# Adding a fixed 256x256 position matrix to an attention product: on VectorE, or on TensorE through the identity

## What is computed

```python
prod2 = jnp.einsum('bnt,btm->bnm', lhs2, rhs2)             # 256x16 times 16x256, per sample
S = jnp.einsum('kj,bij->bik', V_s, jax.nn.sigmoid(prod2 + b_s))   # b_s: 256x256, one for all samples
S = jax.nn.softmax(S, axis=1)
for k in range(3):
    r = jnp.einsum('mn,bmn,bmft->bnft', cheb[k], S, x)
    out = out + jnp.einsum('bnft,fo->bnot', r, Theta[k])
```

## Time and profile before

| what | value |
| --- | --- |
| runs | 702.01, 700.87, 695.55 us; median 700.87 us |
| profiled execution | 696.03 us, span 694.0 us, 12572 instructions |
| mean granted TensorE clock | 0.911 of full |
| busy share of the span | TensorE 80%, weight loads 52%, VectorE 59%, ScalarE 36%, GpSimd 31% |
| L1149, the add of `bs` | 16 times, 678 ns each, 83.2 to 339.7 us |
| L741, the tanh | 16 times, 616 ns each, 83.9 to 342.6 us |
| L459, the product | 64 records, 374 ns each |

### The profile page before, as it was taken

One profiled execution on the slowest core, in us unless ns is written; L12 is line 12 of the kernel. 1 busy time (PEld: TensorE's weight loads), 2 busy tenths in 40 slices (PEclk: granted clock), 3 DMA queues, 4 the chain that ended last, 5 costly groups with the idle time before them and its releaser, 6 DMA issues. The chain is left out here.

```text
span 694.0 us, 12572 instructions
## 1 busy us (share of the span) xinstructions
PE 555.2 (80%) x2488; PEld 362.5 (52%) x2489; DVE 409.3 (59%) x1809; ACT 251.8 (36%) x619; POOL 213.7 (31%) x283
## 2 busy tenths in 40 slices
PE   0567599999999999999985225999999999999243
PEld 0233357766666666666663102666666666665122
DVE  4645236888888888988889771333333333332255
ACT  0343144345544444445442110333333333333232
POOL 5000001224333444443345440334334433443100
PEclk9989599999999999999999556999999999999655
DMA  9900000000000000000001032222222222221597
GB/s 299 421 4 1 0 1 1 0 1 32 31 30 30 31 30 30 30 23 23 27 27 55 31 106 70 77 85 83 84 85 91 78 85 87 91 83 42 164 321 240
DMA packets 36247, 52.69 MB, mean 76 GB/s; under 512 B 4606, under 2 KB 31361, under 8 KB 35969
## 3 DMA queue, kind: packets, MB, share of 16 engines
q1 hardware_dynamic: 24816, 30.86, 14.3%
q0 software_dynamic: 6480, 16.85, 6.5%
q10 hardware_dynamic: 4928, 4.72, 2.1%
HBM read 30.19 MB, written 23.14 MB: 77 GB/s over the span
## 5 line engine op out<-in xcount | busy, mean ns | idle before, releaser
L619 PE MATMUL bank<-w,xT 128*128 x284 | 135.9, 601 | 2.1 <-DVE xT L1420 2.1
L1420 DVE COPY xT<-bank 128x256 f32<-128x256 f32 x71 | 30.2, 425 | 143.8 <-PE bank L606 143.8
L975 POOL DMA_INDIRECT yrows<-xT,dest x71 | 69.4, 978 | 139.4 <-ACT xT L831 135.3
L496 PE MATMUL bank<-work 128*128 128x256 f32 x384 | 93.3, 386 | 0.0
L944 POOL DMA_INDIRECT xrows<-xtok,slot x64 | 64.3, 1005 | 81.4 <-DVEq L1315 66.7
L932 POOL TENSOR_TENSOR yg<-work,sml 128x512 f32<-128x512 f32 x16 | 18.0, 1122 | 196.3 <-DVE work L1225 193.0
L496 PEld LDWEIGHTS bank<-work 128*128 128x128 f32 x384 | 70.4, 190 | 9.0 <-issue 0.8
L634 PE MATMUL bank<-w,xT 128*128 x284 | 73.3, 380 | 1.6 <-ACT xT L836 1.6
L619 PEld LDWEIGHTS bank<-w,xT 128*128 128x128 f32 x284 | 48.8, 192 | 37.6 <-issue 37.6
L825 ACT ACTIVATE xT<-bank 128x256 f32<-128x256 f32 x71 | 27.4, 386 | 94.9 <-PE bank L619 94.9
L634 PEld LDWEIGHTS bank<-w,xT 128*128 128x128 f32 x284 | 48.5, 190 | 6.2 <-issue 2.6
(11 more groups left out here) (203 smaller groups left out, 1017.9 us busy)
## 6 DMA issues: line engine op xcount, KB each, us to landing
xT<-xrows SPq DMA_DIRECT2D x71, 129.0 KB
xT<-yrows SPq DMA_DIRECT2D x32, 256.0 KB, 3.9
xs<-x_in SPq DMA_DIRECT2D x4, 1024.0 KB, 10.8
w<-w13t_in SPq DMA_DIRECT2D x1, 4096.0 KB, 18.3
out<-xT ACTq DMA_DIRECT2D x16, 256.0 KB, 3.7
w<-w2t_in SPq DMA_DIRECT2D x1, 2048.0 KB, 22.7
yrows<-xT,dest POOLq DMA_INDIRECT x71, 2.4
xrows<-xtok,slot POOLq DMA_INDIRECT x64
```

Source lines behind the costliest of these rows:

```text
L496: last = mm(bank[6][:, h * N:(h + 1) * N], z[:, p, c, k, h], A[:, p, c, k], start=(c == 0 and k == 0), stop=(c == C - 1 and k == K - 1))
L619: last = mm(bank[2 + q][:, :], xc[:, q, c], w13[:, e, c].rearrange("p w n -> p (w n)"), start=(c == 0), stop=(c == C - 1))
L975: pool.indirect_dma_start(yrows, bass.IndirectOffsetOnAxis(ap=dest[:, q], axis=0), yo[:, q], None, bounds_check=2 * TOKENS - 1, oob_is_err ...
L1420: V.tensor_copy(xc[:, q].rearrange("p c k -> p (c k)"), bank[q][:, 0:C * P]).then_inc(c_xc, 1)
```

## The change

In `product` each of the two halves of `bank[1]` gets a second matmul: the 128x128 identity times the 128x256 chunk of `bs` opens the accumulation group and the product of `lr` closes it. `add_bs` and its semaphore `b_bs` are gone from VectorE. ScalarE's tanh waits for the product, reads `bank[1]` in PSUM and writes `sg`; it stands ahead of `normalise` in ScalarE's list. The wait on the logits of sample `b-2`, which protects the buffer `sg`, moves from VectorE to ScalarE.

```diff
@@ product, TensorE
                 for c in range(C):
+                    mm(bank[1][:, c * N:(c + 1) * N], ident, bs[:, c], start=True, stop=False)
                     last = mm(bank[1][:, c * N:(c + 1) * N], lr[0:T, p, N + c * P:N + (c + 1) * P],
-                              lr[0:T, p, 0:N], start=True, stop=True)
+                              lr[0:T, p, 0:N], start=False, stop=True)
@@ tanh, ScalarE
             def tanh(b, p):
-                act.wait_ge(s["b_bs"], done(b))
-                nc.scalar.activation(sg[:, p], sg[:, p], ACT.Tanh, scale=0.5).then_inc(s["b_th"], 1)
+                act.wait_ge(s["b_pr"], done(b))
+                act.wait_ge(s["b_L"], done(b - 2))
+                nc.scalar.activation(sg[:, p].rearrange("p c n -> p (c n)"), bank[1][:, :], ACT.Tanh, scale=0.5).then_inc(s["b_th"], 1)
@@ turn, ScalarE
+                if ahead2:
+                    tanh(i + 2, q)
                 if back2:
                     normalise(i - 2, q)
-                if ahead2:
-                    tanh(i + 2, q)
@@ VectorE
-            def add_bs(b, p):
-                dve.wait_ge(s["b_pr"], done(b))
-                dve.wait_ge(s["b_L"], done(b - 2))
-                V.tensor_tensor(sg[:, p].rearrange("p c n -> p (c n)"), bank[1][:, :],
-                                bs[:].rearrange("p c n -> p (c n)"), ALU.add).then_inc(s["b_bs"], 1)
-                yield
@@ matrices in turn, VectorE
                         yield from weigh(i + 1, 1 - q)
-                    if ahead2:
-                        yield from add_bs(i + 2, q)
```

More of the change, by code:

```diff
@@ L246, in build @@
         a_ec = sem("a_ec"); a_rep = sem("a_rep"); a_gh = sem("a_gh")
-        names = ("b_gh b_lr b_pr b_bs b_th b_L b_max b_exp b_rec b_pn b_tr b_A b_z b_zc b_main b_relu b_conv "
+        names = ("b_gh b_lr b_pr b_th b_L b_max b_exp b_rec b_pn b_tr b_A b_z b_zc b_main b_relu b_conv "
                  "b_y b_cen b_sq b_var b_dn b_x1 b_st b_g1 b_q b_g2 b_nb b_xn b_tk b_tkc b_gt b_gtc b_lg "
@@ L992, in _ @@
             V = nc.vector
-            for n in "b_gb b_bs b_max b_rec b_A b_y b_cen b_var b_dn b_st b_q b_nb b_sh b_M b_slot".split():
+            for n in "b_gb b_max b_rec b_A b_y b_cen b_var b_dn b_st b_q b_nb b_sh b_M b_slot".split():
                 dve.sem_inc(s[n], START)
```

## The result

The kernel after takes 710.73 us in the median of four runs (709.12 to 713.29), against 700.66 us for the kernel before in the same comparison: ratio 1.0186, interval 1.0151 to 1.0222. It is slower by 1.9%, about 13 us; the interval holds 2%, so on which side of 2% it lies stays open. The profiled execution took 709.12 us, 13.09 us over the one of before.

A forecast was written before the change was run, and what follows sets the result against it. VectorE's loop was taken to bound steady turns by 0.17 and 0.38 us over TensorE; 1.1 + 2.7 + 0.1 + 0.9 + 3.8 = +8.6 us, added to 698.6, gave 707.2 us, range 700 to 712.

The forecast's parts named there:

- the price of the identity calls: TensorE, each turn's product group: four more matmul records cost 0.90 us, with 0.88 and 1.06 as bounds.
- The third rival: Product group: calls alternating two heights of weights cost the product's 1.06 us; +11.3 us, 709.9 us; chance 0.13.
- Turns -1 to 1: First turns of part B, with no gap on TensorE: 0.9 us more each, +2.7 us.
- turn -2: Start of part B at half clock: 1.8 us for four more records, less 0.7 for the earlier tanh, +1.1 us.
- The steady turn: Turns 4 to 13: +0.26 us in odd turns (18.41) and +0.5 in even (19.23), 3.8 us in all.
- the forecast's loop: Steady turns: route_c through row_max, ScalarE's exps and scale, turn_softmax, features and prefix back to route_c; 18.41 and 19.23 us.
- Turn 2: Part B: TensorE's 0.81 us wait before tokens takes all but 0.1 of the 0.9 us; +0.1 us.
- turn 3: Part B: prefix starts with no wait at all, so the new calls cost their full price, +0.9 us.
- The first rival: Steady turns: VectorE sets the turn and TensorE's gaps take the new calls; -1.8 us, 696.8 us; chance 0.13.
- The second rival: Steady turns: TensorE's own loop alone sets the turn, as scale comes in time; +1.8 us, 700.4 us; chance 0.12.
- The turn is VectorE's loop: Kernel before, steady turns: one route_c to the next sets the turn, by 0.17 us in odd and 0.38 in even turns.
- The tanh: ScalarE: starting off PSUM instead of SBUF, ahead of normalise, costs nothing and is worth nothing in steady turns.

The follow-up runs named there:

- `one_call`: The kernel after with both halves of bs in one identity call of 512 columns ahead of the product calls; ratio to the kernel before 1.0116, about +8 us.
- `both_adds`: The kernel before with the two identity calls added and VectorE's add kept, so bs is added twice; ratio to the kernel before 1.0173.
- `no_add`: The kernel after without the two identity calls, so the position matrix is left out; ratio to the kernel before 0.9904, -6.7 us.
- `after_early`: The kernel after with prefix moved up in TensorE's list to just behind the product; ratio to the kernel before 1.0007.
- `before_early`: The kernel before with prefix moved up in TensorE's list to just behind the product; ratio to the kernel before 0.9978.
- `tanh_late`: The kernel after with the tanh put back behind normalise in ScalarE's list; ratio to the kernel before 1.0151.
- `before_full`: The kernel before with the product over all 128 rows, the added rows being zero; ratio to the kernel before 1.0015.

## Why the prediction was wrong

The direction and the chain of causes came out; the size of the change didn't: 13 us against a sum of 8.6, and against the 6.3 us between the forecast time, 707.2, and the median shown, 700.87. That the measured 710.73 lies in 700 to 712 is luck in part: the ratio of 1.0186 on the comparison's own 700.66 would be 713.7.

- **The step that failed is the price of the identity calls**: "I take 0.90 us a turn, with 0.88 and 1.06 as bounds". Its columns cost the 0.87 of the rows; two more changes of height brought the whole to 3.70 - 2.44 = 1.26 us, outside both bounds. `one_call`, where the same columns come without the two changes (0.86 us), lost 8.1 us, close to the forecast's 8.6. The upper bound was the product's own 1.06, which was read as the price of low calls. It is the price of a group with a change on either side: 0.86 without. The third rival named the alternation but gave it that price too; its sign, a group of 2.1 us and more, was met with 2.41. Turns -1 to 1 show the term bare, 1.12 to 1.25 us each for 0.9. In turn -2, at half clock, the group grew by 2.6 us (4.67 for 2.07) and not by 1.8, which made 1.84 of the expected 1.1.
- **The steady turn was right in kind.** The longer wait of `route_c` (1.6 us for 1.1 to 1.4), `prefix` with no wait ahead of it, L479 waiting for L757 in both kinds of turn and `both_adds` all show the forecast's loop. With 1.26 for 0.90 its sums are 18.77 and 19.59 us for a measured 18.72 and 19.42. The ten turns lost 6.3 us, not 3.8. Turn 2 lost 0.37 for 0.1 and turn 3 1.07 for 0.9; with 1.26 they would be 0.46 and 1.26. The whole sum with 1.26 in it is 14.8 us for a measured 13.1, so what else stands in it is a little too high, by 1.7 us over 16 turns.
- **The first rival** (TensorE's gaps take the calls) fell: `both_adds` equals the kernel after. The Trainium skill's "Perfetto Trace Analysis", section "Identifying the Most-Contended Engine", led to it by reading TensorE at its weight-load share, 67% against VectorE's 89%. VectorE does matter, and its instruction is worth 6.7 us by itself (`no_add`); what decided was TensorE's gap at the place that counts, 0.17 us ahead of `prefix`.
- **The second rival** (TensorE's own loop) is what `after_early` shows once the link is cut, 18.02 and 18.34 us; with the link it doesn't hold.
- **What bounded the kernel before was read in part.** "The turn is VectorE's loop" holds in even turns, with 0.2 us to the next loop; in odd ones the loop through `tokens`, `gn_var`, the root and `normalise` sets it, and VectorE's own list has 0.19 us to spare. VectorE's wait of 0.19 us at L1219 was the sign, and the prediction didn't follow it. This cost the forecast nothing, since the add lies in the root's part of both, but it spoilt the expectation of `before_early`.
- **The tanh** at no cost: right. Its place costs nothing in steady turns (`tanh_late`), and off PSUM it takes 0.60 us where it took 0.62 off SBUF. The reading beside it, a product that ends 2 us ahead of `normalise`, was off (264.33 to 267.93, 3.6 us) and harmless.
- **The base.** The sum was added to 698.6, the mean of four executions, while the median of before in the comparison was 700.66; that took 2 us off the predicted time.

## What to carry to other kernels

Before work is moved to TensorE, look at the heights of the weights on both sides of the place: in this kernel, calls of unlike height that alternate pay 0.19 to 0.20 us at every change, and rows of zeros that make them alike cost TensorE nothing (0.43 us a call either way). A gap in an engine's busy time takes new work only if it lies ahead of the step that others wait for; here moving that step (five small matmuls) gave back 12 us in the kernel after, and 1.5 in the kernel before, where another loop took the rest. Where two loops are nearly equally long, an experiment that shortens one shows nothing until the other is shortened too.

## What the runs showed of the hardware

The price of a change shows in the weight loads. TensorE's weight loads around the group of the kernel after:

```profile
270.57 0.51 PEld L459 LDWEIGHTS bank<-bs,cst 128*128 128x128 f32 x2
271.42 0.29 PEld L460 LDWEIGHTS bank<-lr 16*128 16x128 f32 x2 [0.33 <-issue]
272.04 0.30 PEld L459 LDWEIGHTS bank<-bs,cst 128*128 128x128 f32 x2 [0.33 <-issue]
272.67 0.29 PEld L460 LDWEIGHTS bank<-lr 16*128 16x128 f32 x2 [0.33 <-issue]
```

The first load starts 0.32 us ahead of its matmul at 270.89, beside the matmuls of the features, of the same height. The others follow a change of height: each starts with its matmul, after 0.33 us in which no weights were loaded. The Trainium skill's page "TensorE: Matmul & The Clock Gate", in "Step-by-step: what each phase is for", says that a load is pulled ahead of matmuls in flight when the row groups don't conflict or when it goes to the background buffer, and that the rows of a load don't matter to its time. The second agrees (184 ns for 16 rows, 190 for 128, medians). For the first, no load in these rows ran ahead across a change of height, in either direction, and the load between equal heights did; which of the page's conditions fails is not shown.

"Height" is likely too narrow a name. In the kernel before, far from the product, the weights change in width at full height, and the rows look the same: here `mix` (48 columns of weights) behind `graph` (128), then `gn_mean` (128) behind `mix`.

```profile
257.25 0.59 PEld L452 LDWEIGHTS bank<-xT,ghb 128*48 128x48 f32 x4 [0.33 <-issue]
258.24 0.30 PEld L520 LDWEIGHTS bank<-mv,cst 128*128 128x128 f32 x2 [0.40 <-issue]
```

Both loads start with their matmuls, and the first record of `mix` starts 0.31 us behind the last of `graph`, whose own records are 0.22 apart. The record after a change of height comes with the same 0.33 and 0.31. So any change of the weights' shape may pay; no experiment here took a change of width away.

TensorE's clock fell once in the middle of the loop of `before_full`, after two short waits in a stretch in which it had been busy 16.14 of 18.00 us; four other turns with the same waits kept the full clock. What made this one differ, and whether a quicker TensorE list makes such falls likelier, isn't shown.
